# Two-layer graph network on one core: counting edges ahead of summing them, with the first A·h product inside the edge loop

## The reference, cut to what matters

```
h0 = relu(layernorm(x))
agg[d] = sum over edges e with dst[e] = d of (h0[src[e]] + edge_attr[e])
agg    = (agg @ Wm.T + deg * bm) / max(deg, 1)
o  = h0 + gelu([h0, agg] @ Wu.T + bu)
x1 = x + layernorm(o) * gamma + beta
h1 = relu(layernorm(x1))
r  = (1 + eps) * h1 + sum over edges of h1[src]
out = x1 + h1 + relu(r @ W1 + b1) @ W2 + b2
```

## Time and profile before

| what | value |
|---|---|
| median of the runs | 548.49 us |
| the profiled execution, its time | 548.76 us |
| its span in the profile | 547.0 us |
| TensorE, weight load, VectorE, ScalarE, GpSimd busy | 87%, 51%, 55%, 49%, 20% |
| edge loop, first sums to last turn | 24.1 to 252.1 us |
| first map_agg | 293.2 us |
| first matmul with W1 | 407.6 us |
| DMA rate in the loop | 366 to 396 GB/s |
| load of W1, issue to landing | 12.4 us |

### The profile page before, as it was taken

One profiled execution on the slowest core, in us unless ns is written; L12 is line 12 of the kernel. 1 busy time (PEld: TensorE's weight loads), 2 busy tenths in 40 slices (PEclk: granted clock), 3 DMA queues, 4 the chain that ended last, 5 costly groups with the idle time before them and its releaser, 6 DMA issues.

```text
span 547.0 us, 9240 instructions
## 1 busy us (share of the span) xinstructions
PE 473.7 (87%) x3007; PEld 277.5 (51%) x3007; DVE 300.3 (55%) x849; ACT 265.5 (49%) x599; POOL 107.2 (20%) x100
## 2 busy tenths in 40 slices
PE   4399766788898898764989997989999999999997
PEld 3244433344444444333886555658984445844442
DVE  5555998778998888897384699693210000011111
ACT  7755999988888888894501133423002222200000
POOL 1310010110100000110060267334996000000000
PEclk9599999999999999997999998989999999999999
DMA  8985999989999999994060011000000000011110
GB/s 309 364 317 184 371 411 408 332 356 384 377 383 387 389 386 393 384 385 173 1 213 2 19 36 39 19 20 0 1 1 1 0 0 1 0 38 39 39 38 34
DMA packets 31115, 98.93 MB, mean 181 GB/s; under 512 B 3577, under 2 KB 3577, under 8 KB 31067
## 3 DMA queue, kind: packets, MB, share of 16 engines
q1 hardware_dynamic: 30458, 97.27, 47.5%
q10 hardware_dynamic: 608, 1.05, 0.6%
HBM read 95.76 MB, written 2.56 MB: 180 GB/s over the span
## 4 chain that ended last, share of the span: by engine, by line
PE 61%; DVE 16%; ACT 8%; issue 7%; DVEq 3%; SPq 3%; DMA 1%; POOL 1%; POOLq 0%
PE ps L1185 13%; PE ps L1170 12%; PE ps L1058 6%; PE ps L1059 6%; PE ps L973 6%; PE ps L1076 5%; PE ps L942 5%; ACT square L452 4%; DVE A L653 4%; PE ps L915 3%; DVE aggT L662 2%; DVE U L791 2%; PE ps L961 2%; DVEq L638 2%; ACT X L464 1%
## 5 line engine op out<-in xcount | busy, mean ns | idle before, releaser
L653 DVE TENSOR_TENSOR A<-ps,A 128x120 f32 x316 | 89.5, 283 | 46.6 <-PE ps L953 36.3
L452 ACT ACTIVATE square<-iotaF,T_lo 128x128 bf16<-128x128 f32 x316 | 100.9, 392 | 4.1 <-PE ps L953 3.0
L942 PE MATMUL ps<-ea,oneD 128*24 128x256 f32 x1264 | 84.9, 386 | 20.1 <-issue 8.8
L1058 PE MATMUL ps<-AR,Hh 128*128 128x256 f32 (+1 forms) x280 | 92.4, 354 | 7.1 <-ACT AR L514 5.0
L1059 PE MATMUL ps<-AR,Hl 128*128 128x256 f32 (+1 forms) x280 | 87.9, 338 | 0.0
L886 DVE TENSOR_TENSOR U<-ps,U 128x512 f32<-128x512 f32 (+1 forms) x10 | 6.9, 692 | 128.4 <-PE ps L1185 128.4
L1185 PE MATMUL ps<-W2s,hid 128*128 128x512 f32 (+1 forms) x160 | 68.8, 592 | 0.0
L1170 PE MATMUL ps<-aggT,W1s 128*128 (+1 forms) x192 | 67.3, 513 | 0.0
L1058 PEld LDWEIGHTS ps<-AR,Hh 128*128 128x128 f32 x280 | 55.0, 196 | 14.8 <-ACT AR L514 5.3
L942 PEld LDWEIGHTS ps<-ea,oneD 128*24 128x24 f32 x1264 | 32.5, 103 | 54.0 <-issue 24.5
L1059 PEld LDWEIGHTS ps<-AR,Hl 128*128 128x128 f32 x280 | 54.9, 196 | 6.9 <-issue 1.9
(11 more groups left out here) (134 smaller groups left out, 522.3 us busy)
## 6 DMA issues: line engine op xcount, KB each, us to landing
ea<-in_edge_attr_dram SPq DMA_DIRECT2D x78, 1024.0 KB, 8.6
X<-in_x_dram SPq DMA_DIRECT2D x1, 2304.0 KB
xt<-in_x_dram SPq DMA_DIRECT2D x9, 256.0 KB, 2.7
out_dram<-U SPq DMA_DIRECT2D x9, 256.0 KB
W1s<-in_L_gnn_W_dram SPq DMA_DIRECT2D x1, 2048.0 KB, 12.4
W2s<-in_L_gnn_W_dram SPq DMA_DIRECT2D x1, 2048.0 KB, 11.6
WuN<-in_L_gnn_Wu_dram ACTq DMA_DIRECT2D x1, 1024.0 KB, 5.0
WuN<-in_L_gnn_Wu_dram SPq DMA_DIRECT2D x1, 1024.0 KB, 6.5
```

The lines of the kernel that those rows point to most:

```text
L452: ins = nc.scalar.activation(square[h][:, j, :], iotaF[:], ACT.Square, bias=idxT["lo"][:, j, n:n + 1], scale=-1.0)
L653: V.tensor_tensor(cols, ps[:, 4 + n % 2, j * KW:(j + 1) * KW].rearrange("p (h w) -> p h w", w=W), cols, ALU.add).then_inc(add_step, 1)
L942: last = T.matmul(ps[rows:rows + WS, n % 2, 0:D // 2].rearrange("p (c d) -> p c d", c=2), oneD[h][:, g * 2 + j, :], data, start=j == 0, st ...
L1058: T.matmul(to, Hh[:, c, rows], AR[:, c, start:start + cols], start=start_bank, stop=False)
```

## The change

1. **Spans.** W = 22 for both sums and counts, per 256 edges. A group has two adds to A16 of 10 x 22 columns in place of four of 10 x 12; the two parts of a half accumulate in PSUM. `oneD` is 22 wide, `oneK` 220.
2. **Counts ahead.** The loop counts about four groups in the time of three summed: by n = 58 all 79 are counted (COUNTED, FULL = 58), in 59 loop steps.
3. **One-hots.** ScalarE's square and relu are gone. VectorE makes a counted group's one-hots with eight tensor_scalar compares on a bfloat16 ramp: four of 128 elements and four of 220, each with a per-partition scalar.
4. **Offsets** are loaded one pair at a time, once for the group counted and once for the group summed.
5. **The A·h0 product in the loop.** From n = 60 on each step has a `piece` (8 matmuls of 512 columns for one of the ten blocks): 19 pieces in the loop, one behind it, and the ten of 256 columns between the first map_agg. The fold to degrees and the masked bias go into steps 59 to 78.
6. **Around it.** Three of the products stand ahead of the loop; h0 is made in steps 2 to 11; the moments of x are taken ahead of the loop in one run (10 + 10 instructions); A16 is zeroed by GpSimd. The node order and the two pauses are gone. W1 is loaded when x1 is done, W2 when the layer-2 sums are. The case of counts above 4096 gets its own added product instead of a second set of layers; this input has none.

```diff
-W = 12
-WS = 24
+W = 22
...
+    COUNTED = [min(NG, (4 * (n + 1) + 2) // 3) for n in range(NG)]
+    COUNTS = [list(range(COUNTED[n - 1] if n else 0, COUNTED[n])) for n in range(NG)]
+    FULL = COUNTED.index(NG)
+    H0_AT = list(range(2, 2 + NT))
+    T_AT = [4, 5, 6, 8, 9, 10, 11, 13, 14, 15]
+    U_AT = [7, 12, 16, 21, 26, 32, 37, 42, 47, 52]
...
+    CONV_AT = FULL + 1
+    PIECE_AT = FULL + 2
...
-            sp.dma_start(W1s[:], W1.rearrange("(f p) h -> p f h", p=P)).then_inc(w1_in, 16)
...
+            sp.wait_ge(x1_ready, NT)
+            sp.wait_ge(c_mm, NT)
+            sp.dma_start(W1s[:], W1.rearrange("(f p) h -> p f h", p=P)).then_inc(w1_in, 16)
...
+            nc.gpsimd.memset(A16[:].bitcast(I32), 0).then_inc(counts_zero, 1)
...
             for n in range(NG):
                 packed_copy(n)
-                if n + HOTS < NG:
-                    source_hots(n + HOTS)
...
+                if CONV_AT <= n < CONV_AT + 2 * NT:
+                    piece_conv(n - CONV_AT)
...
-                V.tensor_tensor(oneK[n % HOTS][:], iotaF[:, 0:KW].rearrange("p (a n) -> p a n", a=1).broadcast_to([P, SUB, KW]), n1,
-                                ALU.is_equal).then_inc(hotK_ready, 1)
+            def counts_hots(m):
+                if m >= HOTS:
+                    dve.wait_ge(counts_done, m - HOTS + 1)
+                for j in range(SUB):
+                    V.tensor_scalar(oneS[m % HOTS][:, j, :], iotaB[:, 0:P], idxT["lo"][:, j, m:m + 1], None, ALU.is_equal)
+                for j in range(SUB):
+                    last = V.tensor_scalar(oneK[m % HOTS][:, j, :], iotaB[:, 0:KW], idxT["key"][:, j, m:m + 1], None, ALU.is_equal)
+                last.then_inc(hotK_ready, 1)
...
+            def add_counts(m, half, first):
...
+                if m > 0 or half > 0:
+                    dve.wait_ge(add_step, m * 2 + half)
+                V.tensor_tensor(cols, ps[:, 4 + m % 2, half * KW:(half + 1) * KW].rearrange("p (h w) -> p h w", w=W), cols, ALU.add).then_inc(add_step, 1)
```

The body of VectorE's loop, after:

```diff
+            count_first, sum_first = offsets(0), None
             for n in range(NG):
-                add_counts(n, 0, first[0])
                 if n + HOTS < NG:
                     sums_hots(n + HOTS)
...
+                if n > 0:
+                    sum_first = offsets(n - 1)
+                for m in COUNTS[n]:
+                    for half in range(2):
+                        add_counts(m, half, count_first[half])
+                    if m + 1 < NG:
+                        count_first = offsets(m + 1)
+                    if m + HOTS < NG:
+                        counts_hots(m + HOTS)
...
+                if n > 0:
+                    for half in range(2):
+                        add_sums_of(n - 1, half, sum_first[half])
```

TensorE's loop and tail, after:

```diff
             for n in range(NG):
                 sums(n)
                 if n > 0:
                     turn(n - 1)
-                counts(n)
+                for m in COUNTS[n]:
+                    counts(m)
                 if n in ASIDE:
...
+                if n >= PIECE_AT:
+                    piece(n - PIECE_AT)
             turn(NG - 1)
...
+            map_agg(0)
+            map_agg(1)
+            late(0)
+            map_agg(2)
+            late(1)
+            map_agg(3)
+            map_agg(4)
+            pe.wait_ge(agg_done, 2 * FC + 1)
+            for b in range(5):
+                transpose_h1(b)
+                times_A(b, "A")
+                map_agg(b + 5)
```

More of the change, by code:

```diff
@@ L101, in gnn_kernel @@
[L101 to L118, removed]
@@ L637, in offsets @@
             def offsets(n):
                 _, loaded = nc.values_load_multi_w_load_instructions(
-                    offrow[0:1, n * 8:n * 8 + SUB].bitcast(I32), engines=(mybir.EngineType.DVE,), min_val=0, max_val=(NP << 16) - 1,
-                    skip_runtime_bounds_check_because="each is a pair of least indices of nodes")
-                firsts = []
-                for pair in loaded:
-                    firsts += [pair & 0xFFFF, pair >> 16]
+                    offrow[0:1, n * 4:n * 4 + 2].bitcast(I32), engines=(mybir.EngineType.DVE,), min_val=0, max_val=(NP << 16) - 1,
@@ L792, in _, with extra @@
-            dve.wait_ge(deg_step, 3 + NT)
+            dve.wait_ge(piece_mm, 2 * NT)
+            for f in range(FC):
+                piece_out(1, f)
+            dve.wait_ge(agg_done, 2 * FC)
+            def extra(layer):
+                done = layer * NQ * NT
+                for q, (start, cols) in enumerate(QS):
+                    for c in range(NT):
+                        i = done + q * NT + c
+                        if i > 0:
+                            dve.wait_ge(extra_mm, i)
+                        V.tensor_tensor(rest[:, 0:cols], A16[:, c, start:start + cols], AR[:, c, start:start + cols].bitcast(F32), ALU.subtract).then_inc(extra_ready, 1)
+                    dve.wait_ge(extra_mm, done + (q + 1) * NT)
+                    for f in range(FC):
+                        part = aggT[:, f, start:start + cols]
+                        last = V.tensor_tensor(part, ps[:, CHUNK_BANK[f], 0:cols], part, ALU.add)
+                    last.then_inc(extra_add, 1)
+                dve.wait_ge(extra_add, (layer + 1) * NQ)
@@ L1060, in times_A @@
+                    T.matmul(to, Hh[:, b, rows], AR[:, b, start:start + cols], start=b == 0 and (cols == 512 or f % 2 == 0), stop=False)
+                    last = T.matmul(to, Hl[:, b, rows], AR[:, b, start:start + cols], start=False, stop=b == NT - 1 and (cols == 512 or f % 2 == 1))
                 return last
             def transpose_h1(b):
-                t = ORDER[b]
                 pe.wait_ge(h1_ready, b + 1)
```

1054 lines of the change are left out of this document (535 added, 519 removed).

## The result

The changed kernel takes 644.8 us (median of 4 runs, 643.32 to 646.50) against 548.6 for the kernel before, measured with it: 1.175 times as long, 95% interval 1.172 to 1.179. The profiled execution has a span of 642.7 us. The forecast was 628 with a range of 568 to 660.

The account below looks back on a forecast made before the run. The edge stream sets the pace now; VectorE would set steps 0 to 58 after the change. Terms 30.5 + 272.1 + 13.2 + 3.0 + 59.1 + 1.3 + 246.8 give 626.0 us of span, forecast 628, range 568 to 660.

Parts of the forecast that it names:

- the cheap: Rival, chance 0.23: cheaper compares in the loop, 0.40 us less per counted group, 597 us in all, 568 at the bound.
- the dear rival: Rival, chance 0.09: dearer compares in the loop, 1.68 us per counted group, +28 us, 657 us in all.
- the two halvings: Loop compares: 16 bits halve the 1.04 ns per element, one source in place of two halves it again, 0.26 ns.
- the rival of TensorE's clock: Rival, chance 0.09: a lower TensorE clock adds some 2.5 us in each of ten loop steps, +25 us, 653 us.
- second count add to what follows, across the load: Steps 0 to 58: second count add's start to the first compare, 0.55 plus issue, 0.62 us per counted group.
- second add to `aggT`, `oneD`, load, first count add: Steps 0 to 58, each summed group: this stretch of VectorE's list costs 0.80 us, as in the earlier profile.
- Steps 59 to 78: Loop's end: step 59 takes 3.0 us, then TensorE sets 19 steps of 3.11, 59.1 us; 1.3 to the first map_agg.
- VectorE's pipeline over the blocks is unchanged: Tail from the first map_agg: this pipeline may eat some of the 7 us gained; 5 us either way around 246.8.
- the ring: After the loop: VectorE's update waits for TensorE's map, behind a product awaiting VectorE's split; absent from the forecast, named afterwards.
- the 7 us of lighter work: Tail: nine AB steps lost, 16.6 us, against ten D pieces with half the columns, at least 9.6: -7.0 us.
- The sign: Whole kernel: slower 0.89, faster 0.10, within 0.2% 0.01.
- The rival "faster": Rival, chance 0.10: loads and chained adds hide under other VectorE work, steps 0 to 58 take 157.5 us, 500 in all.

Follow-up runs that it names:

- e2: The changed kernel with the source one-hots undone alone, built on ScalarE again by squares and a relu: 607.4 us.
- e3: The changed kernel with VectorE's register loads of offsets taken out and constants in place of the first columns: 610.1 us.
- e4: The changed kernel with eight throwaway matmuls of 256 columns more on TensorE in each of steps 1 to 59: 649.4 us.
- e1: The changed kernel with TensorE's map of block b+5 moved ahead of its product of block b with A, after the loop: 617.1 us.
- e7: The changed kernel with one load of offsets ahead of the loop, whose two registers every add then uses: 617.0 us.
- e5: The changed kernel with VectorE's instructions reordered, compares, loads and `oneD` standing between chained adds, nothing left out: 613.0 us.
- e8: The changed kernel with offset loads written but constants used; its trace has no load in the loop: 611.6 us.
- e10: The changed kernel with one load of offsets ahead of the loop and a new sum on its registers for each group: 627.8 us.

## Why the prediction was right, and where it was not

**Right: what sets the loop.** The forecast was that VectorE's list, not the stream, would set steps 0 to 58, with a DMA share near 0.6. It is 0.68. e2 and e3 shorten VectorE's list and the loop with it, while e4 raises TensorE's clock and the loop gets no shorter. The compares stood between the cheap and the dear rival, and both fall: start to start the eight took 0.65 + 0.75 = 1.40 us where 1.32 was forecast, and 0.92 (0.56 at the least) and 1.68 by the rivals. From 128 to 220 columns the start of the next moves by (0.75 - 0.65)/4 = 0.025 us, so an element costs 0.025/92 = 0.27 ns, as taken from the two halvings (0.26). The perf-mode tier table of the Trainium skill ("VectorE: DVE Perf Modes") gives four elements per cycle, and the trace agrees with that rate. Its section on the TRN2 errata lists 58 + N/4 cycles, which would have made the eight compares 0.85 us by estimate, and adds itself that the row under-predicts a single instruction; the trace shows 1.40. In the rival of TensorE's clock (+25 us) the clock did fall, to 0.84, but VectorE's waits and e4 leave no room for its price.

**The size of steps 0 to 58 was off, by 24.5 us too much.** All distances from one VectorE start to the next in that stretch, summed from the trace of the changed kernel, against the terms of the forecast:

| term | forecast, us | measured, us |
|---|---|---|
| second count add to what follows, across the load | 79 x 0.62 = 49.0 | 31.3 |
| second add to `aggT`, `oneD`, load, first count add | 59 x 0.80 = 47.2 | 40.1 |
| the eight compares | 79 x 1.32 = 104.3 | 77 x 1.40 = 108.3 |
| two chained adds of counts | 79 x 0.57 = 45.0 | 44.3 |
| two chained adds of sums | 59 x 0.45 = 26.6 | 24.1 |
| Wu1 adds, bias, a register load and branch | 7.6 | 6.9 |
| instructions stretched while GpSimd runs | 5.6 | 5.9 |
| together | 285.3 | 260.9 |

The largest miss is "across the load, 0.62". It rested on a load of 0.52 us that brings four offsets; the one of the change brings two, and its row is

```profile
L615 DVEq TENSOR_LOAD <-offrow x158: 302/309/548, 30.1 to 356.8; - x158
```

At 0.30 us it ends under the second add, and 75 of 77 times the compares follow that add by 0.38 to 0.40 us; twice it was 0.74 and 0.75. The pattern with `oneD` took 150.91 - 150.25 = 0.66 in most steps, where the earlier trace rows had 0.80 for the like, and in the ten steps behind a Wu1 add the load passed under that add, with the count add only 0.16 behind `oneD`. Against these gains stand most of the 7.8 us of waiting for TensorE, which are in the 40.1 and for which the sum had no term. The two chained adds, 0.57, were met, but the reason was wrong: most of the gap is address arithmetic behind the wait and not the wait itself. The one-hots of two groups are made ahead of the loop; the forecast counted them there and once more among its 79, 2.6 us too much. GpSimd's term was met, in another form than forecast: mostly compares are stretched, not one-hots of the sums, and unevenly. Four compares of 220 columns that take 0.83 us elsewhere took 1.95 beside a subtraction:

```profile
61.72 1.95 DVE L611 TENSOR_SCALAR oneK<-iotaB,T_key 128x220 bf16<-128x220 bf16 x4
62.11 1.30 POOL L381 TENSOR_TENSOR Hl<-X,Hh  x1 [6.61 <-ACT Hh L455]
```

Eight of the ten subtractions stretched something, 4.2 us in all; the other 1.7 came in the first compares of the loop, beside GpSimd's work on the indices.

**Steps 59 to 78** took 6.3 us more than the 63.4 forecast. A step with TensorE full has a period of 304.40 - 301.19 = 3.21 us, 0.10 over the forecast, 2 us in all. Two steps stand out. The one from 310.81 to 317.37 took 6.56: it holds the small products for the degrees and `most`, about 2.3 us that the sum had no term for on TensorE, and behind them h0·A matmuls 0.42 apart, at a granted clock of 0.81 in that step. The one from 327.45 to 332.22 took 4.77: TensorE waited 1.0 us for VectorE to empty the banks (L676) before the second ten pieces, and the first matmuls behind were slower. The last piece and the way to the first map_agg took 3.4 us in place of 1.3; against this, the 3.0 us of step 59 fell away, as the sums of step 60 began at 291.55.

**The step that failed** is in the tail: "VectorE's pipeline over the blocks is unchanged", with 5 us either way. VectorE's list of steps is, but for the two pauses and the adds of h0·A between the steps; the order of TensorE's is not. Before, each map of the sums stood ahead of the products with A that wait for VectorE; the change puts the product with A of block b ahead of the map of block b + 5, and VectorE needs that map before it can finish the block whose split the next product waits for. I had costed the instructions that leave the tail and not the order of those that stay. The tail is 281.5 us against 246.8. In e1 it is 615.0 - 360.7 = 254.3, so 27.2 of the 34.7 us are the ring (28.9 up to W1; the part behind was 1.7 longer in that run, as in e2 and e7). Even without the ring the stretch to W1 is 113.1 us, only 1.3 under the 114.4 of before; why the 7 us of lighter work don't come out of it was not tried.

So the span came out 16.7 us over the forecast's 626.0, and the time 17 over 628: -24.5 in steps 0 to 58, +6.3 behind them, +34.7 in the tail and +0.2 at the start. That it came so near is luck, as the two large errors have opposite signs. **The sign** came from the right cause. The rival "faster" has the loads and chained adds under other work, which is what e5's order brings about; but even then the kernel takes 613 us, since VectorE is still busy for 209 of 231 us. The stream's 2.67 us per step, on which the 500 us of that rival rests, needs more than that order.

## What to carry to other kernels

When a change reorders an engine's list, compare its order with every wait of its partner, also in stages where no instruction was added: one line of order cost 28 us here. When work goes to an engine that is second to the bound, compare its sum per step with that of the bound first. Put independent instructions between adds that are chained and whose addresses are worked out anew each time; the wait then passes under them together with the arithmetic behind it. And look into the trace of an experiment for the thing that it was to keep or remove: e7 and e8 had lost what they were to keep.

## What was not expected of the hardware

Two chained VectorE adds with constant addresses run 0.03 us apart (0.39 + 0.39 in 0.81, e3), and so do two whose address stands ready in a register (0.80, e7); without a chain the second starts 0.08 us before the end of the first. With an address that is worked out anew they are 0.17 to 0.18 us apart, without any load (e10). The register operation between them fills the gap, with 0.03 us ahead of it and 0.05 behind: 0.09 us of it at the adds to A16 of the changed kernel, 0.046 at the adds to `aggT` of e10, where two adds took 0.63 us, a gap of 0.14. A load of one word with two offsets held the sequencer for 0.30 us, one of two words for 0.52. In the changed kernel VectorE's 16-bit compares took 0.16 us (128 columns) and 0.19 us (220) each, start to start; beside a GpSimd subtraction of 1.3 us four of them took up to 1.1 us more.
